# Query parts written to DRAM once and repeated by the reads, and Mamba's sums, decays and inputs placed later in the merge of two streams

## What is computed

```
x = x + L0_attn(ln(x));  x = x + L0_xattn(ctx, ln(x));        x = x + L0_ffn(ln(x))
x = x + L1_attn(ln(x));  x = x + L1_xattn(ln(x), ctx, mask);  x = x + L1_ffn(ln(x))
x = x + L2_attn(ln(x));  x = x + L2_xattn(ln(x), ctx);        x = x + L2_ffn(ln(x))
x = x + L3_attn(ln(x));  x = x + L3_xattn(ln(x), ctx);        x = x + L3_ffn(ln(x))
```

```
h[n] = exp(delta * A[n]) * h[n] + (delta * u) * B[n];   y += h[n] * C[n]
```

## Time and profile before

| | |
|---|---|
| median of 3 runs | 4764.98 us (4752.53 to 4768.23) |
| the profiled execution's own time | 4766.72 us |
| its span, first to last instruction | 4764.2 us |
| busy PE, DVE, ACT, POOL | 3496.6, 2955.6, 1970.0, 1234.1 us |
| mean granted PE clock | 0.833 of full speed |
| DMA, mean over the span | 69 GB/s, queue q1 busy 20.1% of 16 engines |

### The profile page before, as it was taken

One profiled execution on the slowest core, in us unless ns is written; L12 is line 12 of the kernel. 1 busy time (PEld: TensorE's weight loads), 2 busy tenths in 40 slices (PEclk: granted clock), 3 DMA queues, 4 the chain that ended last, 5 costly groups with the idle time before them and its releaser, 6 DMA issues. The chain is left out here.

```text
span 4764.2 us, 69288 instructions
## 1 busy us (share of the span) xinstructions
PE 3496.6 (73%) x25546; PEld 2337.3 (49%) x25546; DVE 2955.6 (62%) x6919; ACT 1970.0 (41%) x3470; POOL 1234.1 (26%) x1568
## 2 busy tenths in 40 slices
PE   5868867666878878665886887856589698685674
PEld 3645635334665555433575654533357465352353
DVE  4436874884554785577545488477654548738646
ACT  2423545343343444543344355434235335443333
POOL 0001451550000243253000045145100005516410
PEclk7989978777988988777898998877789799786776
DMA  7110121313121021032122112122211200211321
GB/s 237 46 47 14 39 81 42 103 55 106 66 79 62 28 76 58 29 130 73 47 100 69 39 36 81 45 88 84 104 56 52 98 10 28 80 54 45 117 101 49
DMA packets 174905, 328.00 MB, mean 69 GB/s; under 512 B 13260, under 2 KB 114988, under 8 KB 173740
## 3 DMA queue, kind: packets, MB, share of 16 engines
q1 hardware_dynamic: 174572, 323.59, 20.1%
HBM read 231.87 MB, written 91.67 MB: 68 GB/s over the span
## 5 line engine op out<-in xcount | busy, mean ns | idle before, releaser
L1881 PE MATMUL bank<-sb_big,sb_weights_const 128*128 128x512 f32 x512 | 376.6, 826 | 333.9 <-DVE sb_big L2119 333.2
L1434 POOL TENSOR_TENSOR sb_rs<-sb_ve,sb_weights_const 128x4 f32<-128x4 f32 x112 | 113.4, 1012 | 1757.6 <-DVE sb_ve L1420 1757.3
L1997 POOL TENSOR_TENSOR sb_big<-sb_big 128x512 f32<-128x512 f32 x384 | 496.4, 1307 | 244.9 <-DVE sb_big L2097 244.3
L1958 ACT ACTIVATE bank<-sb_big,sb_Aneg 128x512 f32<-128x512 f32 x512 | 351.7, 689 | 497.4 <-DVE sb_big L2114 392.3
L1252 DVE TENSOR_REDUCE sb_small<-bank 128x4 f32<-128x308 f32 (+1 forms) x512 | 265.9, 523 | 344.5 <-PE bank L967 340.9
L2114 DVE TENSOR_TENSOR_SCAN sb_big<-bank,sb_big 128x512 f32<-128x512 f32 x384 | 464.6, 1210 | 6.6 <-ACT bank L1958 6.3
L988 PE MATMUL bank<-sb_big 128*77 128x128 bf16 (+1 forms) x2560 | 358.1, 234 | 83.7 <-DMA sb_big<-key_parts 30.3
L988 PEld LDWEIGHTS bank<-sb_big 128*77 128x77 bf16 (+1 forms) x2560 | 274.2, 117 | 140.2 <-issue 89.8
L967 PE MATMUL bank<-sb_big 128*128 128x77 bf16 (+1 forms) x2048 | 187.4, 227 | 179.5 <-DMA sb_big<-query_parts 114.2
L1677 PEld LDWEIGHTS bank<-sb_weights_L1f,sb_big 128*128 128x128 f32 x2048 | 257.3, 191 | 109.0 <-issue 104.9
L1137 ACT ACTIVATE sb_big<-bank 77x512 f32<-77x512 f32 (+1 forms) x352 | 207.9, 593 | 228.3 <-PE bank L1009 152.4
(11 more groups left out here) (344 smaller groups left out, 8111.7 us busy)
## 6 DMA issues: line engine op xcount, KB each, us to landing
sb_big<-query_parts SPq DMA_DIRECT2D x160, 512.0 KB, 6.5
sb_big<-state_rows SPq DMA_DIRECT2D x128, 512.0 KB, 3.8
query_parts<-sb_big SPq DMA_DIRECT2D x120, 384.0 KB, 3.3
sb_big<-key_parts SPq DMA_DIRECT2D x64, 512.0 KB, 8.9
sb_big<-context_key_parts SPq DMA_DIRECT2D x64, 308.0 KB, 3.6
key_parts<-sb_big SPq DMA_DIRECT2D x48, 384.0 KB, 4.1
context_key_parts<-sb_big SPq DMA_DIRECT2D x48, 231.0 KB, 4.1
sb_big<-masked_key_parts SPq DMA_DIRECT2D x32, 308.0 KB, 3.5
```

Of the source, the lines that this page charges most:

```text
L1881: pe.matmul(m.bank[s][2][:, :], m.const["ident"], M.h(s, 2 * (n % 2)), start=n == 0, stop=n == NS - 1)\
L1958: act.activation(M.dA(s, half), M.dl(s, half), ACT.Exp, scale=m.Aneg[:, NS * half + n:NS * half + n + 1])\
L1997: pool.tensor_tensor(M.h(s, 2 * (n % 2) + half), M.b_rows(s, n // 2)[:, n % 2, :], M.du(s, half), ALU.mult)\
```

## The change

It has three parts. **Queries:** their parts are written once (24 rows), and each of the four reads of a group repeats these rows three times into rows 0 to 71 of the stack; rows 72 to 127 come in four reads of their own (224 KB each) that don't wait for the write. The key parts keep their three writes, in another order of rows. **Mamba:** PE's sum moves from 0.6 to 0.9 of a state, ACT's decays from 0.4 and 0.9 to 0.6 and 1.1 of the state before, POOL's inputs from 0.2 and 0.6 to 0.4 and 0.8. **Semaphores:** one more is needed for the landing of the rows below (`rp`), and the four of the last sublayer (`qf_*`) are folded into existing ones; the waits keep their meaning. The renaming is left out below.

```diff
 def stacks(u):
+    if u == 0:
+        pe.wait_ge(*g.landed("rp", (A.key, 3)))
     if u % 4 == 0:
         pe.wait_ge(*g.landed("rq%d" % (u // 4), A.key))
         pe.wait_ge(*g.landed("rk%d" % (u // 4), A.key))
...
 def heads_write_sp(sp, g, m, A, name):
     sp.wait_ge(*g.at("proj_d", (A.key, name, "low")))
-    dst = A.dram(s, name)[0:USED].rearrange("(i j d) h n -> (d h) i j n", i=3, j=3)
+    if name == "q":
+        dst = A.dram(s, name)[0:3 * DH].rearrange("(i d) h n -> (d h) i n", i=3)
+        sp.dma_start(dst, A.parts(s, name)).then_inc(*g.landing("wq", A.key))
+        for group in range(4):
+            h = slice(4 * group, 4 * group + 4)
+            sp.dma_start(A.q(s)[USED:A.rows, h, :], A.dram(s, name)[USED:A.rows, h, :])\
+              .then_inc(*g.landing("rp", (A.key, group)))
+        return
+    dst = A.dram(s, name)[0:USED].rearrange("(j i d) h n -> (d h) i j n", i=3, j=3)
     for copy in range(3):
-        sp.dma_start(dst[:, :, copy, :] if name == "q" else dst[:, copy, :, :], A.parts(s, name))\
-          .then_inc(*g.landing("w" + name, (A.key, copy)))
+        sp.dma_start(dst[:, copy, :, :], A.parts(s, name)).then_inc(*g.landing("wk", (A.key, copy)))
...
 def heads_read_sp(sp, g, m, A, name):
     for group in range(4):
         h = slice(4 * group, 4 * group + 4)
         for each in name:
-            stack = A.q(s) if each == "q" else A.k(s)
-            sp.dma_start(stack[0:A.rows, h, :], A.dram(s, each)[0:A.rows, h, :])\
-              .then_inc(*g.landing(f"r{each}{group}", A.key))
+            if each == "q":
+                rows = A.dram(s, each)[0:3 * DH, h, :].rearrange("r h n -> r (h n)")
+                sp.dma_start(A.q(s)[0:USED, h, :].rearrange("p h n -> p (h n)"),
+                             rows[None, :, :].to_broadcast([3, 3 * DH, rows.shape[1]]))\
+                  .then_inc(*g.landing(f"rq{group}", A.key))
+            else:
+                sp.dma_start(A.k(s)[0:A.rows, h, :], A.dram(s, each)[0:A.rows, h, :])\
+                  .then_inc(*g.landing(f"rk{group}", A.key))
...
-            yield M.scan_at(way, n, 0.6)
+            yield M.scan_at(way, n, 0.9)
...
-                yield M.at(way, 0.13) if n == 0 else M.scan_at(way, n - 1, 0.4 + 0.5 * half)
+                yield M.at(way, 0.13) if n == 0 else M.scan_at(way, n - 1, 0.6 + 0.5 * half)
...
-                yield M.at(way, 0.115) if n == 0 else M.scan_at(way, n - 1, 0.2 + 0.4 * half)
+                yield M.at(way, 0.115) if n == 0 else M.scan_at(way, n - 1, 0.4 + 0.4 * half)
```

More of the change, by code:

```diff
@@ L219 @@
     sc_in="Pool: a state's input", sc_y1="Pool: state added to the second half's y",
-    qf_pe="PE: quantised network", qf_a="ACT: quantised network", qf_d="DVE: quantised network",
-    qf_p="Pool: quantised network",
 )
@@ L227 @@
     rb1="an odd pair of rows of B is on all partitions",
+    rp="the rows below the query parts are in the stack",
     wq="query parts are in DRAM", wk="key parts are in DRAM", wm="the masked keys' row is in DRAM",
@@ L1364, in heads_read_sp @@
     for each in name:
-        sp.wait_ge(*g.landed("w" + each, (A.key, 2)))
+        sp.wait_ge(*g.landed("w" + each, A.key if each == "q" else (A.key, 2)))
     for group in range(4):
@@ L2239, in quantised_pe @@
         pe.matmul(m.bank[s][k][:, :], Q.w("w1", 128 * j, 128 * j + 128), m.xT[s][:, :], start=True, stop=True)\
-          .then_inc(*g.one("qf_pe", ("h", j)))
-        free[s, k] = ("qf_a", ("h", j))
+          .then_inc(*g.one("ff_pe", ("h", j)))
+        free[s, k] = ("ff_a", ("h", j))
     for b in range(NB + 1):
@@ L2251, in quantised_pe @@
                                     m.const["ident"])
-            last.then_inc(*g.one("qf_pe", ("tok", b)))
-            free[s, b % 2] = ("qf_d", ("q1", b))
+            last.then_inc(*g.one("ff_pe", ("tok", b)))
+            free[s, b % 2] = ("ff_d", ("q1", b))
         if b >= 1:
             yield Q.time(b - 1, 0.8)
-            pe.wait_ge(*g.at("qf_d", ("q3", b - 1)))
+            pe.wait_ge(*g.at("ff_d", ("q3", b - 1)))
             g.wait_free(pe, free, s, 2)
@@ L2260, in quantised_pe @@
                                     Q.qb(s, b - 1)[:, 128 * j:128 * j + 128], m.identb[:, :])
-            last.then_inc(*g.one("qf_pe", ("back", b - 1)))
-            free[s, 2] = ("qf_a", ("qT", b - 1))
+            last.then_inc(*g.one("ff_pe", ("back", b - 1)))
+            free[s, 2] = ("ff_a", ("qT", b - 1))
     yield 0.98
     g.wait_free(pe, free, s, 3)
-    pe.wait_ge(*g.at("qf_a", ("qT", NB - 1)))
+    pe.wait_ge(*g.at("ff_a", ("qT", NB - 1)))
     for b in range(NB):
@@ L2269, in quantised_pe @@
                              m.w2t[:, 128 * j:128 * j + 128], start=j == 0, stop=j == 3)
-    last.then_inc(*g.one("qf_pe", "out"))
+    last.then_inc(*g.one("ff_pe", "out"))
     free[s, 3] = ("x_upd", "L3f")
@@ L2299, in quantised_pool @@
             last = pool.memset(Q.hp(s, j)[:, :, at:at + 1], 0.0)
-    last.then_inc(*g.one("qf_p", "pad"))
+    last.then_inc(*g.one("proj_p", "pad"))
 def quantise_tokens_dve(dve, g, m, Q):
@@ L2307, in step @@
     def step(name, last):
-        last.then_inc(*g.one("qf_d", name))
+        last.then_inc(*g.one("ff_d", name))
     def after(name):
-        dve.wait_ge(*g.at("qf_d", name))
+        dve.wait_ge(*g.at("ff_d", name))
     yield 0.02
@@ L2353, in quantised_dve @@
             if tap == 0:
-                dve.wait_ge(*g.at("qf_a", ("h", j)))
-                dve.wait_ge(*g.at("qf_p", "pad"))
+                dve.wait_ge(*g.at("ff_a", ("h", j)))
+                dve.wait_ge(*g.at("proj_p", "pad"))
                 ins = dve.tensor_scalar(Q.hs(s, j), src, w, None, ALU.mult)
             else:
-                dve.wait_ge(*g.at("qf_d", ("conv", j, tap - 1)))
+                dve.wait_ge(*g.at("ff_d", ("conv", j, tap - 1)))
                 ins = dve.scalar_tensor_tensor(out=Q.hs(s, j), in0=src, scalar=w, in1=Q.hs(s, j),
                                                op0=ALU.mult, op1=ALU.add)
-            ins.then_inc(*g.one("qf_d", ("conv", j, tap)))
+            ins.then_inc(*g.one("ff_d", ("conv", j, tap)))
     for b in range(NB):
         def step(name, last):
-            last.then_inc(*g.one("qf_d", (name, b)))
+            last.then_inc(*g.one("ff_d", (name, b)))
         def after(name):
-            dve.wait_ge(*g.at("qf_d", (name, b)))
+            dve.wait_ge(*g.at("ff_d", (name, b)))
         yield Q.time(b, 0.0)
-        dve.wait_ge(*g.at("qf_pe", ("tok", b)))
+        dve.wait_ge(*g.at("ff_pe", ("tok", b)))
         step("mx", dve.tensor_reduce(Q.sm(s, 4, b), m.bank[s][b % 2][:, :], AX.X, ALU.max))
@@ L2395, in quantised_dve @@
         if b >= 2:
-            dve.wait_ge(*g.at("qf_pe", ("back", b - 2)))
+            dve.wait_ge(*g.at("ff_pe", ("back", b - 2)))
         step("q3", dve.tensor_scalar(Q.qb(s, b), Q.qa(s, b), ROUND, None, ALU.subtract))
     yield 0.96
-    dve.reciprocal(Q.sm(s, 8), Q.sm(s, 7)).then_inc(*g.one("qf_d", "inv2"))
-    dve.wait_ge(*g.at("qf_d", "inv2"))
-    dve.tensor_scalar(Q.sm(s, 8), Q.sm(s, 8), m.wsc[:, 3:4], None, ALU.mult).then_inc(*g.one("qf_d", "f"))
+    dve.reciprocal(Q.sm(s, 8), Q.sm(s, 7)).then_inc(*g.one("ff_d", "inv2"))
+    dve.wait_ge(*g.at("ff_d", "inv2"))
+    dve.tensor_scalar(Q.sm(s, 8), Q.sm(s, 8), m.wsc[:, 3:4], None, ALU.mult).then_inc(*g.one("ff_d", "f"))
     yield 0.99
-    dve.wait_ge(*g.at("qf_d", "f"))
-    dve.wait_ge(*g.at("qf_pe", "out"))
+    dve.wait_ge(*g.at("ff_d", "f"))
+    dve.wait_ge(*g.at("ff_pe", "out"))
     for b in range(NB):
```

16 lines of the change are left out of this document (8 added, 8 removed).

## The result

The changed kernel takes 4915.36 us (median of 4 runs, 4909.56 to 4921.27) where the kernel before, run beside it on the same chip, takes 4764.48: a ratio of 1.0321, 95% interval 1.0299 to 1.0343, so 3.2% slower. The sign and the range held; the size did not: +151 us against +80 in the forecast. The profiled execution took 4909.56 us, its span is 4907.8.

A forecast was written before the change was run, and what follows sets the result against it. No engine or queue was taken to bound throughout, only waits, with DVE the bound in the scans. Costs of 19 + 42 + 39 + 38 = 138 us, 110 taken, with the merge's -30 gave +80: 4845 us median, range 4762 to 4930.

The forecast's parts named there:

- Three engines: Repeated query reads: each is cut into 3 shares, so 96 KB per engine and 3.9 us per read.
- the 138 of the sum: Whole queries' part: 19 queries alone, 42 with keys, 39 seam, 38 behind the reads; 138 us, of which 110 taken.
- The rival on 12 engines: Repeated reads spread over 12 engines, first group landing at 6.8 us instead of 8.9: faster, 4705 us; chance 0.13.
- The reads of the rows below: Four reads issued during the write: 896 KB on at most 14 engines, 2.6 us, landed some 5.8 us after the start.
- the queries alone: Sublayers reading queries without keys, 24 places: +0.9 us in 14 places, 6 us for second groups; sum 19 us.
- the pairs: Queries read with keys (L0a, L3a, 16 places): a pair takes 5.2 us instead of 2.6; sum 42 us.
- the seams: Seam of two passes, three times: stream 1's first product waits 24.7 us instead of 11.7, +13 each, 39 us.
- The cover: Part of the queries' waits falls where the other stream has work queued ahead: 110 us taken of 138.
- What stands behind the reads: DMAs queued after the query reads, such as B's rows in Mamba, land later: sum 38 us.
- The merge: Mamba's scans: a third of PE's share of DVE's waits is won, -30 us; loss bounded by +20.
- The covered case: Three engines, but waits mostly covered and a merge that works: 4765 us; chance 0.10.
- The slow case: Three engines with a slower share (4.5 us per read), or a merge that starves the scan: 4950 us; chance 0.07.

The follow-up runs named there:

- e3: The changed kernel with each repeated read replaced by three reads of 24 rows: 4774.58 us, ratio 1.0045 to the kernel before.
- e5: The kernel before plus ten bursts of eight reads behind its last store, by partitions read: 4890.85 us; per read 1.32 us for 0-127, 1.16 for 72-127.
- e2: The kernel before with Mamba's merge as changed and the queries as before: 4695.26 us, ratio 0.9872.
- e9: The changed kernel with the rows below read group by group, each repeated read left as one DMA: 4903.92 us, ratio 1.0305 to the kernel before.
- e7: The kernel before with only Mamba's sums on PE moved, from 0.6 to 0.9 of a state: 4702.93 us, ratio 0.9884.
- e8: The kernel before with only ACT's decays (0.4 to 0.6) and POOL's inputs (0.2 to 0.4) moved: 4752.92 us, ratio 0.9998.
- e4: As e3, but rows below read group by group, group 0's behind the write, later ones ahead of their group's reads: 4731.17 us, ratio 0.9948 to the kernel before.

## Why the prediction was right in sign and too small

**Three engines: right.** 3.6 to 3.8 us between the landings in the kernel and 3.8 by itself, where 3.9 was forecast. Experiment e3 puts their price at some 130 us, near the 138 of the sum, which is nearly all theirs. The rival on 12 engines is out; experiment e3 is a form of it, with reads of 0.5 us in place of one of 3.9, and runs at 4775.

**The reads of the rows below: the step that failed.** "896 KB on at most 14 engines, 64 KB each, 2.6 us, landed some 5.8 us after the start": they went over 14 engines, but took 1.2 to 1.3 us each, as much as a full read, and landed at 8.5. I had priced bytes per engine, and looked only at the engines; the price goes by which rows are read (experiment e5), and that it is the side of SBUF that sets it rests on the page named there. The 2.7 us between 5.8 and 8.5 stand in every place where PE waits. Put into the terms of the sum they give: 14 x 2.7 = 38 for the queries alone, 11 x 2.7 = 30 for the pairs, which stand behind the keys' writes, and with the seams (17.5 us each by PE's three waits, not 13) 13, so 138 becomes 219. By the result and experiment e2 the queries' part costs 214 on top of the merge, and the added 81 stand beside the 79 that experiment e3 leaves to other causes than the three engines. The places bear it out: by the timelines the first product now comes 12.5 to 13.1 us after the write at the L1x and at stream 0's L3x (8.8 to 9.0 before, 9.8 forecast), and 20.1 to 21 at the pairs (14.7 to 15 before). That the two totals agree so closely is partly luck, since the single terms are good to a few us. How much of the loss would go if the rows below alone were not read, with three engines kept, no run shows, and experiment e9 warns that it could be less.

**The cover: not borne out.** "Of which I take 110": a discount of 28 us with no row behind it. By the sum above nothing is left that was covered; no run tests it by itself.

**The seams: 46.3 us of wait against the 42 forecast.** The mechanism held, with stream 1's rows below, which landed over 6 us after stream 0's first repeated read was issued, and a first read issued 1.6 us later on top.

**What stands behind the reads: right.** POOL waits for B's rows at 11 places, and the scan's idle time that POOL's input ended is 43.3 us in all, beside the 38 of the sum.

**The merge: right in sign, half in size.** -30 against -59 alone. I had taken a third of the DVE waits that PE ended; the scan stretches gave 13.2 us per pass, of 38.6 that they had. Of the three moves only PE's counts (experiments e7, e8). The waits fit this reading: the sum had stood at PE's head waiting for DVE's product with the other stream's matmuls behind it. The 392 us of ACT, which I named beside the 333 of PE, were worth nothing. This error and the one of the queries partly cancel: the queries' part cost 104 us more than I took, the merge gave some 30 more. That the time still fell within the range owes to that.

**The rivals.** The covered case had the better estimate of the merge and the wrong one of the cover. The slow case (4950) was 35 us off, my number 70; but its reason, a slower repeated read, did not occur.

## What to carry to other kernels

Price a DMA by what each of its sides allows: how many engines the cut gives it, and how its partitions spread over SBUF; 56 rows at 72-127 cost nearly what 128 do, and a repetition in the outermost place ran on as many engines as it has copies. A saving of bytes on a queue that fills a fifth of the time is worth nothing by itself: 31 MB less went with 151 us more. A small read set ahead of the one waited for can cost its full price (43 us between e3 and e4). An engine that waits in order should be given the waiting instruction late: but only the engine that others queue behind, and not so late that it holds up what stands behind it.
